# Cross-attention with a mixture-of-experts layer: the second k product moved directly behind the first in TensorE's order

## The chip, the cores and the metric

One core of one Trainium2 chip runs the whole program. The metric is the device time of one execution in microseconds (us); the median of three runs of the kernel before is 1068.2 us (1066.75 to 1069.43).

## The reference, cut to what matters

The input x is 16 batches of 256 tokens by 512. Each batch attends to its own context of 256 tokens by 256: 240 ordinary tokens and 16 further ones (DCA) that have their own weights and their own softmax. There are 16 heads of 32. The queries, and the keys, are normalised head by head. Then a layer with 6 experts follows, of which each batch uses 2.

```python
q = _ln((x @ Wq + bq).reshape(b, s1, H, HD), qn_w, qn_b)
kv = jnp.concatenate([y_main @ Wk + bk, y_main @ Wv + bv], axis=-1)
kv = kv.reshape(b, s2, H, 2 * HD)
k = _ln(kv[..., :HD], kn_w, kn_b)
v = kv[..., HD:]
ctx = _attn(qT, k.transpose(0, 2, 1, 3), v.transpose(0, 2, 1, 3))
ctx_dca = _attn(qT, k_dca.transpose(0, 2, 1, 3), v_dca.transpose(0, 2, 1, 3))
x = x + (ctx + ctx_dca) @ Wo + bo
x = x + ffn(_layernorm(x))       # gate on the batch's mean, 2 of 6 experts
```

## The kernel before, in words

**Two phases.** The function attention_phase works through the 16 batches one after the other, and ffn_phase then does the experts. The change lies in the first.

**A software pipeline.** In one step of the attention phase, TensorE does the attention of batch b, and between its pieces the projections (q, k, v) of batches ahead, so that the other engines have time to work on the scores. The function walk (line 328) lists the steps: p0, p1, p2 fill the pipeline; first, body (eleven times), close and late have both attention and projections; later, last and tail empty it. So there are fourteen steps in which attention (attn) and projections (proj) are both done. The Python function body (line 745) of the TensorE program is the order of TensorE's work, written out by hand. Each engine has such an order of its own and takes its instructions strictly in that order; semaphores make one engine wait for another.

**The attention of a batch.** First come eight groups of scores (line 679, matmuls at line 687) with the queries on the partitions; VectorE takes their maxima (line 1012), ScalarE their exponentials and sums (line 844). From the sums a shift for each query and head is made: VectorE (line 1121), TensorE transposes it (line 692, LT), VectorE splits it into s_hi and s_lo (lines 1123 and 1125), and two DMAs (line 377; s_hi issued by SyncE, s_lo by ScalarE) lay it as additional rows under the stacked queries QS. Then the scores are computed a second time, transposed and with the shift already in them: eight groups scores_t 0 to 7 (line 699, matmuls at line 708). I call them T0 to T7. T0 waits until both DMAs have landed (line 702). Each Tp fills one of two double-bank buffers, sc[p % 2], with four matmuls, and must wait until ScalarE has emptied that buffer (line 704). ScalarE empties it with one activation, exp, into pt (probabilities, line 855, activation at line 860): exps 0 to 7. Behind T3, T5 and T7 stand products of the probabilities with the values (line 713, matmuls at line 723), here P0, P1, P2, and at the end of the step P3.

**The k products.** project_kv(step, b, c, 0) computes half c of the key rows: K0 (128 rows) and K1 (112 rows), each of six matmuls of 512 columns (line 653), because the operands are split in a high and a low part. Results go to one of four PSUM banks (ring). K0 has bank 3, K1 has bank 0; the unit that used bank 0 ahead of K1 is LT. VectorE adds the bias and takes a bank's result away (bias_k, line 1061). ScalarE squares it (line 835), VectorE sums the squares (line 976), GpSimd takes the root (line 509) and normalises k (line 533); TensorE transposes it in the next step (line 674), before that step's fourth group of scores. ScalarE's order at this place is: exp 0, exp 1, square of K0, exp 2, exp 3, square of K1, exp 4, exp 5, exp 6, exp 7. VectorE's is: bias of K0, normalise first half of q (line 984), bias of K1, sum of K0's squares, normalise second half of q, result of P0 (line 1079), sum of K1's squares.

Of the kernel before, what the change touches and what calls it, by code (L numbers as in the profile page):

```python
# [169 lines left out]
def attention_phase(nc, stack, early, moe, x, ctx, Wq, bq, Wk, bk, Wv, bv, Wdca, bdca, qn_w, qn_b, kn_w, kn_b,  # L170
# [140 lines left out]
    def begin(eng, step, name, b):  # L311

        wait(eng, evac[u.bank(step, name)], u.count(step, name, b))
        return ring[u.bank(step, name)]
# [10 lines left out]
    def wait_evac(eng, step, name, b):  # L325
        eng.wait_ge(evac[u.bank(step, name)], u.count(step, name, b) + 1)
# [36 lines left out]
    def kv_half(columns, half):  # L363

        return columns.rearrange("p (h w) -> p h w", w=W)[:, :, half * HD:(half + 1) * HD]
# [212 lines left out]
    def _(pe):  # L578
# [33 lines left out]
        def x_transposes(step, b):  # L612
            pe.wait_ge(xh_rdy, T * (b + 3))
            for j in range(2):
                bank = begin(pe, step, f"XT{j}", b)
                for k in range(2):
                    for t in range(T):
                        last = pe.transpose(bank[:, (k * T + t) * P:(k * T + t + 1) * P],
                                            xh[:, t, (2 * j + k) * P:(2 * j + k + 1) * P], ident[:, :])
                last.then_inc(full[u.bank(step, f"XT{j}")], 1)  # L620

        def context_transposes(step, b):
            pe.wait_ge(c_ld, 16 * (b + 3))
            bank = begin(pe, step, "CT", b)
            for cc in range(CC):
                for c in range(NC):
                    last = pe.transpose(bank[:, cc * TOK + c * P:cc * TOK + (c + 1) * P],
                                        cin[:, c, cc * P:(cc + 1) * P], ident[:, :])
            last.then_inc(full[u.bank(step, "CT")], 1)

        def project_q(step, b, t):
            bank = begin(pe, step, f"Q{t}", b)
            wait_evac(pe, step, "XT0", b)
            wait_evac(pe, step, "XT1", b)
            if step == "p1":
                pe.wait_ge(prep, 2)
            for kc in range(KC):
                last = pe.matmul(bank[:, :], xT[:, kc, t * P:(t + 1) * P], wq[:, kc, :],  # L638
                                 start=(kc == 0), stop=(kc == KC - 1))
            last.then_inc(full[u.bank(step, f"Q{t}")], 1)  # L640

        def project_kv(step, b, c, half):

            name = "KV"[half] + str(c)
            bank = begin(pe, step, name, b)
            if half == 0:
                wait_evac(pe, step, "CT", b)
                if step == "p1":
                    pe.wait_ge(wkv_rdy, 2)
            parts = [(cc, c_part, w_part) for cc in range(CC)  # L650
                     for c_part, w_part in ((cT, wkv_hi), (cT, wkv), (cT_lo, wkv_hi))]
            for n, (cc, c_part, w_part) in enumerate(parts):
                last = pe.matmul(bank[0:ROWS[c], :], c_part[:, cc, c * P:c * P + ROWS[c]],
                                 kv_half(w_part[:, cc, :], half),
                                 start=(n == 0), stop=(n == len(parts) - 1))
            last.then_inc(full[u.bank(step, name)], 1)
# [11 lines left out]
        def k_transposes(step, b):  # L668
            pe.wait_ge(k_norm, NC * (b + 2))
            for j in range(2):  # L670
                bank = begin(pe, step, f"KT{j}", b)
                for g in range(2):
                    for c in range(NC):
                        last = pe.transpose(bank[:, g * TOK + c * P:g * TOK + c * P + ROWS[c]],
                                            kb[0:ROWS[c], c, (2 * j + g) * P:(2 * j + g + 1) * P],
                                            ident[0:ROWS[c], 0:ROWS[c]])
                last.then_inc(full[u.bank(step, f"KT{j}")], 1)

        def scores(b, par, k):

            if k == 0:
                pe.wait_ge(q_in, STACKED * (b + 1))
                pe.wait_ge(k_in, STACKED * (b + 1))
            wait(pe, sc_evac[k % 2], 8 * b + k // 2)
            t, quad = k // G, k % G
            for i in range(HP):
                last = pe.matmul(sc[k % 2][:, i // 2, (i % 2) * TOK:(i % 2 + 1) * TOK],  # L687
                                 QS[par][0:BLK, i, quad, t * P:(t + 1) * P], KS[par][0:BLK, i, quad, :],
                                 start=True, stop=True)
            last.then_inc(sc_full[k % 2], 1)  # L690

        def shift_transposes(step, b):
            bank = begin(pe, step, "LT", b)
            pe.wait_ge(lt_rdy, b + 1)
            for t in range(T):
                last = pe.transpose(bank[0:2 * H, t * P:(t + 1) * P], lt[:, t, :], ident[:, :])
            last.then_inc(full[u.bank(step, "LT")], 1)
# [31 lines left out]
        def out_projection(step, b, t, half):  # L729

            if half == 0:
                if step in ATTN:
                    pe.wait_ge(ctx_rdy, b)
                else:
                    wait_evac(pe, "last", "PV3", B - 1)
                bank = begin(pe, step, f"WO{t}", b)
            else:
                bank = ring[u.bank(step, f"WO{t}")]
            for g in (2 * half, 2 * half + 1):
                last = pe.matmul(bank[:, :], ot[:, g, t * P:(t + 1) * P], wo[:, g, :],  # L740
                                 start=(g == 0), stop=(g == G - 1), skip_group_check=True)
            if half == 1:
                last.then_inc(full[u.bank(step, f"WO{t}")], 1)

        def body(step, b, par):
            attn, proj, keyed, wout = step in ATTN, step in PROJ, step in KEYED, step in WOUT
            if attn:
                scores(b, par, 1)
            if keyed:
                project_kv(step, b, 0, 1)  # L750
            if attn:
                scores(b, par, 2)
            if keyed:
                project_kv(step, b, 1, 1)
                k_transposes(step, b)
            if attn:
                scores(b, par, 3)
            if wout:
                out_projection(step, b, 0, 0)
            if attn:  # L760
                scores(b, par, 4)
            if wout:
                out_projection(step, b, 0, 1)
            if attn:
                scores(b, par, 5)
            if wout:
                out_projection(step, b, 1, 0)
            if attn:
                scores(b, par, 6)
            if proj:  # L770
                x_transposes(step, b)
            if attn:
                scores(b, par, 7)
            if proj:
                project_q(step, b, 0)
                context_transposes(step, b)
            if wout:
                out_projection(step, b, 1, 1)
            if attn:
                shift_transposes(step, b)  # L780
            if proj:
                project_q(step, b, 1)
            if proj:
                project_kv(step, b, 0, 0)
            if attn:
                scores_t(b, par, 0)
                scores_t(b, par, 1)
            if proj:
                project_kv(step, b, 1, 0)
            if attn:  # L790
                scores_t(b, par, 2)
                scores_t(b, par, 3)
                values(step, b, par, 0)
                scores_t(b, par, 4)
                scores_t(b, par, 5)
                values(step, b, par, 1)
            if step == "p1":
                project_dca()
            if step == "p2":
                dca_k_transposes()  # L800
                scores(0, 0, 0)
            if proj:
                q_transposes(step, b)
            if attn:
                scores_t(b, par, 6)
                scores_t(b, par, 7)
                values(step, b, par, 2)
            if step in AHEAD and attn:
                scores(b + 1, 1 - par, 0)
            if attn:  # L810
                values(step, b, par, 3)
            if step == "p2":
                pe.wait_ge(wo_ld, 32)

        walk(pe, body)


# [846 lines left out]
```

## Time and profile before

| what | value |
|---|---|
| median of 3 runs | 1068.2 us (1066.75 to 1069.43) |
| the profiled execution | 1067.38 us |
| its span, first to last instruction | 1065.5 us, 17588 instructions |
| mean granted TensorE clock | 0.951 |
| TensorE matmuls busy | 926.1 us (87%) |
| TensorE weight loads busy | 658.8 us (62%) |
| VectorE busy | 765.5 us (72%) |
| ScalarE busy | 595.5 us (56%) |
| GpSimd busy | 393.8 us (37%) |
| steps with attention and projections | 14, from some 110 to 650 us |

The profiled execution gives the durations; its own time lies 0.8 us below the median of the runs. Engines in its rows: PE is TensorE's matmuls, PEld its weight loads, DVE VectorE, ACT ScalarE, POOL GpSimd, SP SyncE; a q behind a name means the engine's sequencer (a DMA issue, for example). "L653" is line 653 of the kernel. "x8" is the number of instructions merged in a row. What stands in square brackets is idle time of that engine before the row, and what ended it.

### The profile page before, as it was taken

Reading aid. Unit: us, or ns where it says so; the run is one execution under the profiler, and the core shown is the slowest. Engines: PE = TensorE matmul, PEld = TensorE weight load, DVE = VectorE, ACT = ScalarE, POOL = GpSimd, SP = SyncE. Lnnn points to the kernel's source line nnn. Section 1 sums busy time; section 2 is a strip of 40 time slices with the busy share of each in tenths; the row PEclk is TensorE's granted clock in tenths of the full one; section 3 lists DMA queues with packets and bytes.
Section 4 is the critical chain, followed back from the end, with each engine's and each line's share of the span. In section 5 each row is a group of like instructions: output and inputs, shape, how many; then the busy total and the mean of one; then the engine's idle time right before and its main releaser. Section 6 shows DMA issues by size and latency. Waiting matters only on the chain. (4 is left out here: it accounts for less than half of the span.)

```text
span 1065.5 us, 17588 instructions
## 1 busy us (share of the span) xinstructions
PE 926.1 (87%) x5148; PEld 658.8 (62%) x5148; DVE 765.5 (72%) x1723; ACT 595.5 (56%) x1627; POOL 393.8 (37%) x277
## 2 busy tenths in 40 slices
PE   3673999999999999999999997764599999999998
PEld 1343656556556655655655654432489999898997
DVE  6644788778777778777777776334877878878784
ACT  1134778678778678678678778554422323223231
POOL 4627537537536636636636744000000000000000
PEclk9796999999999999999999999777699999999999
DMA  9236455464464364365364355367011111111111
GB/s 273 39 81 152 109 128 136 122 145 123 115 157 118 107 170 114 98 170 119 92 172 117 90 147 120 96 239 234 1 60 60 59 56 42 59 59 59 59 39 40
DMA packets 54588, 116.54 MB, mean 109 GB/s; under 512 B 11992, under 2 KB 20568, under 8 KB 54296
## 3 DMA queue, kind: packets, MB, share of 16 engines
q1 hardware_dynamic: 53416, 115.29, 39.2%
q10 hardware_dynamic: 816, 0.79, 0.3%
q0 software_dynamic: 320, 0.02, 0.2%
q8 instruction: 18, 0.29, 0.1%
q14 instruction: 18, 0.15, 0.0%
HBM read 47.24 MB, written 17.30 MB: 61 GB/s over the span
## 5 line engine op out<-in xcount | busy, mean ns | idle before, releaser
L509 POOL TENSOR_TENSOR vs<-vs,neg_half 128x16 f32<-128x16 f32 x66 | 195.9, 2982 | 185.4 <-DVE vs L978 185.2
L851 ACT ACTIVATE sc<-sc,nm 128x240 f32<-128x240 f32 x512 | 225.8, 456 | 31.5 <-DVE ed L1023 31.5
L1018 DVE TENSOR_REDUCE pm<-sc 128x64 f32<-128x1024 f32 x128 | 156.4, 1222 | 49.9 <-PE sc L687 46.3
L860 ACT ACTIVATE pt<-sc 128x1024 f32<-128x1024 f32 x128 | 124.2, 1024 | 44.6 <-PE sc L708 44.6
L687 PE MATMUL sc<-KS,QS 96*128 96x256 f32 x512 | 99.4, 318 | 46.7 <-ACT sc L851 34.9
L1475 ACT ACTIVATE hb<-hb 128x352 f32<-128x352 f32 x64 | 31.9, 498 | 186.9 <-DVE hb L1531 186.8
L687 PEld LDWEIGHTS sc<-KS,QS 96*128 96x128 f32 x512 | 72.2, 194 | 101.8 <-ACT sc L851 75.8
L638 PE MATMUL ring<-wq,xT 128*128 128x512 f32 x256 | 121.3, 618 | 15.7 <-DVE q L1056 7.4
L740 PE MATMUL ring<-wo,ot 128*128 128x512 f32 x256 | 121.0, 597 | 0.7 <-DVE ot L1079 0.7
L851 ACT ACTIVATION_READ_ACCUMULATOR sc<-sc,nm 128x1 f32 x512 | 117.0, 229 | 0.0
L708 PE MATMUL sc<-QS,KS 100*128 100x256 f32 x512 | 82.6, 305 | 13.7 <-DMA QS<-s_lo 13.1
L708 PEld LDWEIGHTS sc<-QS,KS 100*128 100x128 f32 x512 | 70.7, 200 | 32.2 <-DMA QS<-s_lo 12.2
L638 PEld LDWEIGHTS ring<-wq,xT 128*128 128x128 f32 x256 | 47.8, 197 | 68.4 <-issue 55.9
L1349 PE MATMUL f_ring<-w_hi,f_xT_hi 128*128 x256 | 84.8, 331 | 2.6 <-DVE f_xT_lo L1513 2.6
L1405 PE MATMUL f_ring<-w_hi,hT_hi 128*128 (+1 forms) x192 | 80.7, 420 | 5.9 <-DVE w_lo L1503 5.7
L1349 PE MATMUL f_ring<-w_hi,f_xT_lo 128*128 x256 | 84.1, 328 | 0.0
L1349 PE MATMUL f_ring<-w_lo,f_xT_hi 128*128 x256 | 83.9, 328 | 0.0
L1405 PE MATMUL f_ring<-w_lo,hT_hi 128*128 (+1 forms) x192 | 76.1, 396 | 0.0
L1405 PE MATMUL f_ring<-w_hi,hT_lo 128*128 (+1 forms) x192 | 75.9, 395 | 0.0
L723 PE MATMUL ring<-pt,v 128*32 128x256 f32 x1024 | 70.6, 394 | 0.6 <-ACT pt L860 0.6
L1079 DVE TENSOR_SCALAR ot<-ring,bv_p 128x256 f32<-128x256 f32 x64 | 30.7, 479 | 50.9 <-PE ring L723 50.9
L1335 POOL TENSOR_TENSOR gd<-euler,gd 128x1 f32<-128x1 f32 x16 | 8.8, 552 | 156.4 <-DVE gd L1611 156.4
(154 smaller groups left out, 1858.3 us busy)
## 6 DMA issues: line engine op xcount, KB each, us to landing
QS<-q_hi SPq DMA_DIRECT2D x128, 128.0 KB, 2.3
KS<-k_hi SPq DMA_DIRECT2D x128, 128.0 KB, 2.4
xin<-in_x_dram SPq DMA_DIRECT2D x16, 512.0 KB, 3.6
QS<-q_lo SPq DMA_DIRECT2D x64, 128.0 KB, 2.3
KS<-k_lo SPq DMA_DIRECT2D x64, 128.0 KB, 2.3
xres<-in_x_dram SPq DMA_DIRECT2D x16, 512.0 KB, 3.2
x_scratch<-xres SPq DMA_DIRECT2D x16, 512.0 KB, 3.8
x<-x_scratch SPq DMA_DIRECT2D x16, 512.0 KB, 3.2
```

The costliest lines, as they stand in the source:

```text
L509: pool.tensor_tensor(w, w, neg_half[0:rows, :], ALU.pow).then_inc(rstd, 1)
L638: last = pe.matmul(bank[:, :], xT[:, kc, t * P:(t + 1) * P], wq[:, kc, :], start=(kc == 0), stop=(kc == KC - 1))
L687: last = pe.matmul(sc[k % 2][:, i // 2, (i % 2) * TOK:(i % 2 + 1) * TOK], QS[par][0:BLK, i, quad, t * P:(t + 1) * P], KS[par][0:BLK, i, qu ...
L708: last = pe.matmul(sc[p % 2][:, i, c * S:(c + 1) * S], KS[par][:, h, g, c * P:(c + 1) * P], QS[par][:, h, g, :], start=True, stop=True)
L723: last = pe.matmul(bank[i * HD:(i + 1) * HD, 0:S], v[par][:, c, h * HD:(h + 1) * HD], pt[g % 2][:, i, c * S:(c + 1) * S], start=(c == 0), ...
L740: last = pe.matmul(bank[:, :], ot[:, g, t * P:(t + 1) * P], wo[:, g, :], start=(g == 0), stop=(g == G - 1), skip_group_check=True)
L851: last = act.activation(s, s, ACT.Exp, bias=nm[:, t, h:h + 1], accum_out=den[:, t, h:h + 1])
L860: act.activation(pt[g % 2][:, (p % 2) * 2:(p % 2) * 2 + 2, :], sc[p % 2][:, :, :], ACT.Exp).then_inc(sc_evac[p % 2], 1)
L1018: dve.tensor_reduce(pieces, s.rearrange("p h (c n) -> p h c n", n=DCA), AX_X, ALU.max, negate=True).then_inc(g_max, 1)
L1349: last = pe.matmul(bank[:, 0:FF], xT[xp][:, kc, t * P:(t + 1) * P], w1[wp][:, bass.ds(ex[e], 1), kc, :].rearrange("p a f -> p (a f)"), sta ...
L1405: last = pe.matmul(bank[:, :], hT[hp][0:rows, e, fc, t * P:(t + 1) * P], w2[wp][0:rows, bass.ds(ex[e], 1), fc, :].rearrange("p a n -> p (a ...
L1475: act.activation(hb[:, n, :], hb[:, n, :], ACT.Gelu).then_inc(h_rdy, 1)
```

## The change

Two lines are moved: project_kv(step, b, 1, 0), that is K1, comes directly behind K0 and ahead of T0. So the order K0, T0, T1, K1, T2, T3 becomes K0, K1, T0, T1, T2, T3. Nothing else changes: neither the work, nor the banks, nor the semaphores' counts, nor the order of another engine. In p1 and p2, which have no attention, K1 was behind K0 already.

```diff
             if proj:
                 project_kv(step, b, 0, 0)
+                project_kv(step, b, 1, 0)
             if attn:
                 scores_t(b, par, 0)
                 scores_t(b, par, 1)
-            if proj:
-                project_kv(step, b, 1, 0)
-            if attn:
                 scores_t(b, par, 2)
                 scores_t(b, par, 3)
                 values(step, b, par, 0)
```

## Rows read from the trace of the kernel before

**Rows 1.** The page: TensorE's busy time, and its granted clock in 40 slices

```profile
PE 926.1 (87%) x5148; PEld 658.8 (62%) x5148; DVE 765.5 (72%) x1723; ACT 595.5 (56%) x1627; POOL 393.8 (37%) x277
...
PEclk9796999999999999999999999777699999999999
```

**Rows 2.** Busy time in two whole steps: stretch, length, PE, PEld, DVE, ACT, POOL, clock

```profile
392.60:431.93 39.33, 37.03 (x215) 22.90 (x214) 30.61 (x66) 30.28 (x88) 22.11 (x12) 1.00 0.50 129
431.93:471.67 39.74, 37.03 (x215) 22.86 (x214) 30.24 (x66) 30.28 (x88) 22.08 (x12) 1.00 0.50 128
```

**Rows 3.** Groups of instructions, 110 to 640 us: busy us, mean ns, idle before

```profile
L860 ACT ACTIVATE pt<-sc 128x1024 f32<-128x1024 f32 x110 | 106.7, 1025 | 23.3 <-PE sc L708 23.3
...
L708 PE MATMUL sc<-QS,KS 100*128 100x256 f32 x440 | 66.9, 292 | 3.6 <-DMA QS<-s_lo 3.5
...
L1061 DVE TENSOR_TENSOR kb<-ring,bkv_b 128x512 f32<-128x512 f32 (+1 forms) x28 | 19.3, 690 | 7.4 <-PE ring L653 7.4
```

**Rows 4.** Timeline of TensorE, one step: start us, duration us, what

```profile
435.46 0.40 PE L653 MATMUL ring<-wkv_hi,cT_lo 128*128 128x512 f32 x1
436.47 1.21 PE L708 MATMUL sc<-QS,KS 100*128 100x256 f32 x8 [0.61 <-DMA QS<-s_lo]
437.51 0.40 PE L653 MATMUL ring<-wkv_hi,cT 128*112 128x512 f32 x1
...
438.71 0.40 PE L653 MATMUL ring<-wkv_hi,cT_lo 128*112 128x512 f32 x1
438.94 1.10 PE L708 MATMUL sc<-QS,KS 100*128 100x256 f32 x8
439.98 1.07 PE L723 MATMUL ring<-pt,v 128*32 128x256 f32 x16
440.98 1.36 PE L708 MATMUL sc<-QS,KS 100*128 100x256 f32 x8
```

**Rows 5.** Timeline of ScalarE: the issue of s_lo's DMA in three consecutive steps

```profile
392.60 0.63 ACTq L377 DMA_DIRECT2D QS<-s_lo  x1
...
431.93 0.63 ACTq L377 DMA_DIRECT2D QS<-s_lo  x1
...
471.67 0.63 ACTq L377 DMA_DIRECT2D QS<-s_lo  x1
```

**Rows 6.** Timeline of TensorE: T0 and T1 of the step before that of rows 4

```profile
396.71 1.22 PE L708 MATMUL sc<-QS,KS 100*128 100x256 f32 x8 [0.18 <-DMA QS<-s_lo]
```

**Rows 7.** Timeline of ScalarE in the step of rows 4

```profile
437.24 1.94 ACT L860 ACTIVATE pt<-sc 128x1024 f32<-128x1024 f32 x2 [1.07 <-PE sc L708]
439.07 0.63 ACT L835 ACTIVATE sq<-kb 128x512 f32<-128x512 f32 x1
439.62 1.94 ACT L860 ACTIVATE pt<-sc 128x1024 f32<-128x1024 f32 x2
441.44 0.63 ACT L835 ACTIVATE sq<-kb 112x512 f32<-112x512 f32 x1
441.96 1.95 ACT L860 ACTIVATE pt<-sc 128x1024 f32<-128x1024 f32 x2
```

**Rows 8.** Timeline of TensorE in the step late: K0's last matmul, then T0

```profile
632.27 0.40 PE L653 MATMUL ring<-wkv_hi,cT_lo 128*128 128x512 f32 x1
632.54 1.22 PE L708 MATMUL sc<-QS,KS 100*128 100x256 f32 x8
```

**Rows 9.** K1's consumers after rows 4: VectorE, GpSimd, k's transposes (first to last start)

```profile
439.14 0.69 DVE L1061 TENSOR_TENSOR kb<-ring,bkv_b 112x512 f32<-112x512 f32 x1 [0.83 <-PE ring L653]
...
440.71 6.14 POOL L509 TENSOR_TENSOR vs<-vs,neg_half 128x16 f32<-128x16 f32 x2 [0.63 <-DVE vs L978]
446.93 2.06 POOL L533 TENSOR_TENSOR kb<-kb,vs 128x512 f32<-128x512 f32 x2
...
L674 PE MATMUL ring<-ident,kb x8: 260/267/274, 452.6 to 453.3; 128*128 128x128 f32 x4, 112*128 112x112 f32 x4
```

**Rows 10.** Timeline of TensorE in the step later, which has no projections

```profile
670.29 2.08 PE L708 MATMUL sc<-QS,KS 100*128 100x256 f32 x8 [4.87 <-DMA QS<-s_lo]
```

## The prediction

> **What bounds the kernel now.** I began with the page. It shows TensorE's matmuls busy for 87% of the span [rows 1], which tempts one to take TensorE for the bound everywhere. The change acts only where attention and projections are mixed, in fourteen steps, so I next asked for whole steps, cut from one issue of the DMA of s_lo to the next. In both, TensorE is busy for 37.03 us and ScalarE for 30.28 us, yet one lasts 39.33 us and the other 39.74 us [rows 2]. The work is the same and the length is not: something that is no engine's work decides 0.41 us.
>
> The timelines of the two steps show what. In the first, T0 starts at 396.71, which is 4.11 us after the issue of s_lo at 392.60; in the second it starts at 436.47, 4.54 us after the issue at 431.93 [rows 4 to 6]. T0 is 0.43 us later in the second, and that step is 0.41 us longer. In both, the wait that ends last ahead of T0 is the landing of s_lo. So a delay of T0 goes through to the end of the step one to one. That is the central reading: **the start of T0 is on the path**, for all that TensorE looks nearly full.
>
> ScalarE's timeline shows why. It idles 1.07 us for T0's result; then it runs exps 0 and 1, the square of K0, exps 2 and 3, the square of K1 and exps 4 and 5 with no idle time between the rows [rows 7]. Whatever moves exp 0 moves this whole train. T5 can start only when exp 3 has emptied its buffer, and everything in TensorE's order behind T5 follows.
>
> **The change part by part.**
>
> K1 ahead of T0. Its six matmuls start at 437.51, and the next matmul behind them starts at 438.94 [rows 4]: 1.43 us for the six, 0.24 us for each. In fourteen steps that is 14 x 1.43 = 20.0 us put ahead of T0. The operands of K1 are those of K0 but for the rows, and both banks are free. LT, which used bank 0 before, was taken away by VectorE before s_lo's DMA could be issued, 3.5 us before K0's last matmul starts [rows 4, 5], so I expect no wait ahead of K1.
>
> For one matmul of 512 columns I take the row's 0.24 us. The Trainium skill, page "TensorE: Matmul & The Clock Gate", section "Back-to-back issue gap", gives 518 cycles at 2.4 GHz, that is 0.216 us; by it K1 would cost 1.30 us and the sum would come out 1.8 us lower. The pitch measured here is longer, so the measurement decides.
>
> What K1 covers. While TensorE waits for s_lo's landing it can now do K1. In all steps together TensorE idles 3.6 us ahead of line 708 [rows 3], and I counted such a wait in eleven of the fourteen steps. The idle time is counted from the modelled end of K0's last matmul, 0.40 us after its start, whereas a following matmul may start 0.24 us after it, as T2 does behind K1 (438.71 to 438.94 [rows 4]). So each of the eleven waits is really 0.16 us longer: 11 x 0.16 = 1.8 us. The three steps without idle time (one is the step late [rows 8], where T0 starts 0.27 us after K0's last matmul) add some 0.3 us. Covered in all: 3.6 + 1.8 + 0.3 = 5.7 us. The rest of K1, 20.0 - 5.7 = 14.3 us, delays T0: 1.02 us in the mean step. After the change no step should wait for s_lo: K1 ends 1.43 us after the point where T0 could start at the earliest, and the longest wait seen is 0.61 + 0.16 = 0.77 us [rows 4].
>
> What K1's old slot gives back. T2 started 2.47 us after T0 and K1 stood ahead of it. T2 needs sc[0], which exp 0 empties: exp 0 starts at 437.24 and lasts 1.025 us [rows 3, 7], so T2 could start at about 438.3 instead of 438.94, 0.6 us earlier. That helps only if exp 2 was waiting for T2. ScalarE had its own train: exp 1, then the square of K0, then exp 2. The square to the next exp takes 0.55 us here (439.07 to 439.62) and 0.52 us at the second square (441.44 to 441.96) [rows 7]; the difference, 0.03 us, is all that exp 2 can have waited. The price is bounded by 0 and by 14 x 0.6 = 8.5 us; I take 14 x 0.03 = 0.4 us, since ScalarE shows no idle time there, and keep the other end for a rival.
>
> New waits. T2 now waits for exp 0 and T3 for exp 1, where K1 used to fill the time; together they idle TensorE for as much as K1 no longer fills, about 1 us. Queued behind T2 and T3 are P0, T4 and T5. P0 needs exp 1 and T4 needs exp 2, which the delayed train ends later in any case, so this costs nothing further. If ScalarE's train were shorter, P0 and T4 would be late next.
>
> K1's consumers. VectorE idled 0.83 us for K1 in this step [rows 9], 7.4 us in all [rows 3]. The bias of K1 now comes earlier, but VectorE's next instruction, the sum of K0's squares, needs ScalarE's square of K0, which comes 1 us later. GpSimd's roots start after that, so they shift by the same 1 us. I cost this at nothing. The cover is large: GpSimd ends with k at 448.99, and the transposes that need it start at 452.6 [rows 9], 3.6 us later; they shift too. No DMA is moved: SyncE's and ScalarE's issues of s_hi and s_lo come before, and the loads in SyncE's queue behind them depend on K0, K1, T0 in nothing.
>
> The sum: 20.0 - 5.7 - 0.4 = **13.9 us slower**. On the profiled execution's own 1067.38 us this gives 1081.3 us; the median of the runs stands 0.8 us above that execution, so I predict 1068.2 + 13.9 = 1082.1 us, 1.3% longer. The steps outside the fourteen, and the experts' phase, keep their length and shift as a whole.
>
> **The rivals.**
>
> Faster: TensorE is the bound of the whole step. Then the only thing that counts is its idle time, and K1 fills 5.7 us of it: 1068.2 - 5.7 = 1062.5 us. For it speaks the busy share, 37.03 of 39.33 us [rows 2]. It would decide if TensorE had no idle time behind T1, so that pulling K1 out of there advanced everything by K1's full 1.43 us; it turns to a gain from a relief of 1.02 us per step on. Against it: T2 cannot start before exp 0 ends, so the relief is at most 0.6 us, and a later T0 lengthened the step one to one though TensorE had the same work. The Trainium skill, page "Perfetto Trace Analysis", section "Identifying the Most-Contended Engine", says that matmul busy time is no good measure of TensorE's headroom and the busy share of weight loads a better one; that share is 22.90 of 39.33 us here, which speaks against this rival too. Chance 0.02.
>
> Partial relief: exp 2 was in truth paced by T2, and ScalarE's row hides it. Then 8.5 us come back instead of 0.4: 20.0 - 5.7 - 8.5 = 5.8 us slower, 1074 us. Against it stands the 0.55 beside the 0.52 us. Chance 0.04.
>
> No change: the delay is absorbed, because another chain (the next step's keys or stacked queries) ends the step just as late. Then 1068 us. Against it: the one-to-one lengthening between T0 and the next step, and a longer delay makes any other chain less binding, not more. That K1 still runs where it was isn't possible, as TensorE's order is the program's. Chance 0.02.
>
> The clock falls: TensorE's pauses grow, and in late parts of the trace its granted clock fell from the upper level (2.4 GHz) to the lower (1.2 GHz) [rows 1]. There the engine had sat idle for up to 4.87 us at a time [rows 10]. In the fourteen steps the new pauses are some 0.5 us each and the clock was granted in full [rows 2]. If each step lost, by a halved clock, its T0 to P0 stretch once more (3.5 us from T0 to P0 [rows 4]), that would be 14 x 3.5 = 49 us: 1131 us. Chance 0.02.
>
> **How the numbers follow.** The forecast has a chance of 0.90. Its own uncertainty: the six matmuls could be 1.30 us rather than 1.43 (-1.8 us), the first and the last of the fourteen steps might pass on less (-2 us), the handing over at T2 and T3 might cost 0.1 us per step (+1.4 us), and the runs scatter by 1.3 us. This gives 1078.5 to 1085 us, and what is left out of the range is less than 2 in 10. A difference under 0.3%, 3.2 us, is about what a measurement can't tell from no change. Slower by more than that: forecast, partial relief and clock, 0.96, from which I take 0.02 for what I have not thought of: 0.94. Faster 0.03, the same 0.03.
>
> **What would show it.** Right, if in the changed kernel the wait for s_lo ahead of line 708 is gone in all fourteen steps; T0 starts some 1.67 us (0.24 + 1.43) after the start of K0's last matmul in every step alike, which is 5.20 us after the issue of s_lo (435.46 - 431.93 + 1.67); the body steps all have nearly one length, 39.33 + (5.20 - 4.11) = 40.4 us; ScalarE's idle time ahead of exp 0 has grown by 1 us per step, from 1.07 to 1.7 us in the step read above [rows 7]; exps 0 to 5 keep their distances; small idle times appear on TensorE ahead of T2 and T3, ended by exp; and VectorE's 7.4 us for K1 are gone. Wrong, if exp 2 follows T0 by clearly less than the 3.15 us of now (439.62 - 436.47), if the steps keep their length though T0 is later, or if the granted clock shows a dip within the fourteen steps.

## The result, and the profile after

The changed kernel took 1082.55 us in the median of four runs (1080.23 to 1085.41), against 1068.59 us for the kernel before, measured beside it: a ratio of 1.0138, with a 95% interval of 1.0117 to 1.0159. That is 14.0 us more; 13.9 us were predicted. That the two agree to 0.1 us is luck, since the interval reaches from 12.5 to 17.0 us. The profiled execution took 1080.23 us, 12.85 us more than the one of before. Two executions of the experiments stand far outside the others, 1112.71 us in experiment 1 and 1849.24 us in experiment 5: the ratios leave them out, the medians don't.

What comes ahead of the fourteen steps scatters from run to run (they began between 117.2 and 122.1 us in the profiles of this study), so I also compare the fourteen steps alone: from the first issue of s_lo's DMA to the fifteenth. This is the view of one source line, line 377 of ScalarE, cut off behind the fifteenth issue; the last two times of a row are the first and the last start. First the kernel before, then the changed one.

```profile
L377 ACTq DMA_DIRECT2D QS<-s_lo x15: 621/627/757, 117.8 to 666.3; - x15
```

```profile
L377 ACTq DMA_DIRECT2D QS<-s_lo x15: 622/627/757, 117.9 to 679.3; - x15
```

The fourteen steps grew from 548.5 to 561.4 us, by 12.9 us. The whole difference of the profiled executions lies in them.

Whole steps of the changed kernel (columns as in [rows 2]):

```profile
399.78:440.06 40.28, 37.35 (x215) 23.08 (x214) 30.62 (x66) 30.23 (x88) 22.09 (x12) 1.00 0.49 126
440.06:480.32 40.26, 37.34 (x215) 23.08 (x214) 30.22 (x66) 30.21 (x88) 22.09 (x12) 1.00 0.49 126
```

Both last 40.3 us. The lengths that differed by 0.41 us in [rows 2] are now one, because nothing varies any more ahead of T0. The clock was granted in full. Over the whole fourteen steps, 117.9 to 679.3 us, the same view gives 1.00 too, and the page has a 9 (90% or more) in every slice from the fifth to the twenty-fifth:

```profile
PE 930.5 (86%) x5148; PEld 660.7 (61%) x5148; DVE 765.8 (71%) x1723; ACT 594.5 (55%) x1627; POOL 394.1 (37%) x277
...
PEclk9886999999999999999999999768689999999999
```

The groups that answer to [rows 3], 110 to 655 us (line 858 is line 860 of before, 1059 is 1061):

```profile
L858 ACT ACTIVATE pt<-sc 128x1024 f32<-128x1024 f32 x111 | 107.9, 1031 | 37.3 <-PE sc L708 37.3
L708 PE MATMUL sc<-QS,KS 100*128 100x256 f32 x448 | 72.7, 296 | 11.5 <-ACT pt L858 11.5
...
L1059 DVE TENSOR_TENSOR kb<-ring,bkv_b 128x512 f32<-128x512 f32 (+1 forms) x28 | 19.2, 687 | 0.0
```

TensorE no longer waits for s_lo; it waits 11.5 us for exps instead. VectorE's 7.4 us for K1 are gone. ScalarE's idle time ahead of exps 0 and 6 is 37.3 us. The 23.3 us of [rows 3] come from a window that ends before the last of the fourteen steps does; over exactly the fourteen steps it was 24.3 us. So it grew by 13.0 us, as much as the steps did: what the change added is idle time, not work.

TensorE in one step, behind [rows 4]:

```profile
443.58 0.40 PE L653 MATMUL ring<-wkv_hi,cT_lo 128*128 128x512 f32 x1
443.82 0.40 PE L653 MATMUL ring<-wkv_hi,cT 128*112 128x512 f32 x1
...
445.00 0.40 PE L653 MATMUL ring<-wkv_hi,cT_lo 128*112 128x512 f32 x1
445.24 1.11 PE L708 MATMUL sc<-QS,KS 100*128 100x256 f32 x8
447.00 0.74 PE L708 MATMUL sc<-QS,KS 100*128 100x256 f32 x4 [0.64 <-ACT pt L858]
447.91 0.74 PE L708 MATMUL sc<-QS,KS 100*128 100x256 f32 x4 [0.18 <-ACT pt L858]
448.58 1.07 PE L723 MATMUL ring<-pt,v 128*32 128x256 f32 x16
```

T0 starts 1.66 us after the start of K0's last matmul, and the two new waits stand ahead of T2 and T3, 0.82 us together. ScalarE in the same step, behind [rows 5, 7]:

```profile
440.06 0.63 ACTq L377 DMA_DIRECT2D QS<-s_lo  x1
...
445.92 1.94 ACT L858 ACTIVATE pt<-sc 128x1024 f32<-128x1024 f32 x2 [1.61 <-PE sc L708]
447.74 0.63 ACT L833 ACTIVATE sq<-kb 128x512 f32<-128x512 f32 x1
448.26 1.94 ACT L858 ACTIVATE pt<-sc 128x1024 f32<-128x1024 f32 x2
450.07 0.65 ACT L833 ACTIVATE sq<-kb 112x512 f32<-112x512 f32 x1
450.59 1.96 ACT L858 ACTIVATE pt<-sc 128x1024 f32<-128x1024 f32 x2
```

T0 starts 5.18 us after the issue of s_lo (445.24 - 440.06). Exp 0 follows T0 by 0.68 us, against 0.77 us in [rows 4, 7]; exp 2 follows exp 0 by 2.34 us, against 2.38 us. Exp 2 thus follows T0 by 3.02 us instead of 3.15 us; the prediction had named a clearly smaller distance as a sign that it was wrong, and this is a small part of that.

### The profile page after: what moved, and what is told of

Its sections match the earlier page's. It is cut to its first block and busy times, and to the rows that moved or that the text cites. A ratio compares the mean times of both kernels' runs of the same rounds, so it can differ in the third digit from the quotient of the medians.

```text
span 1078.4 us, 17588 instructions
## 1 busy us (share of the span) xinstructions
PE 930.5 (86%) x5148; PEld 660.7 (61%) x5148; DVE 765.8 (71%) x1723; ACT 594.5 (55%) x1627; POOL 394.1 (37%) x277
## 5 line engine op out<-in xcount | busy, mean ns | idle before, releaser
L740 PE MATMUL ring<-wo,ot 128*128 128x512 f32 x256 | 122.1, 601 | 0.7 <-DVE ot L1077 0.7
L708 PE MATMUL sc<-QS,KS 100*128 100x256 f32 x512 | 86.6, 306 | 21.5 <-ACT pt L858 12.0
L974 DVE TENSOR_REDUCE vs<-sq 128x16 f32<-128x512 f32 x66 | 45.0, 681 | 40.5 <-ACT sq L833 40.4
```

Source lines behind the costliest of these rows:

```text
L708: last = pe.matmul(sc[p % 2][:, i, c * S:(c + 1) * S], KS[par][:, h, g, c * P:(c + 1) * P], QS[par][:, h, g, :], start=True, stop=True)
L974: dve.tensor_reduce(w, squares(n, values), AX_X, ALU.add).then_inc(var_rdy, 1)
```

## The experiments

**1 and 2. K1 cut to one matmul, at the old and at the new place.** Both kernels have this edit; one is made in the kernel before, the other in the changed one. Most of k's second half is left out in them.

```diff
-                project_kv(step, b, 1, 0)
+                project_kv(step, b, 1, 0, cut=attn)
...
+            if cut:
+                parts = parts[:1]
```

> K1 is cut from six matmuls to one in the fourteen steps, at its old place behind T1 (so most of k's second half is left out). My theory: the old slot lies beside ScalarE's train of exps and costs nothing there; T2 can start 0.6 us earlier but exp 2 only 0.03 us earlier, so about 0.4 us less than the kernel before, 1067.8 us. Rival 'TensorE is the bound': five matmuls of 0.24 us in fourteen steps go, 16.7 us less, 1051.5 us. Rival 'partial relief' (exp 2 paced by T2): 0.6 us a step, 1060 us.

> K1 is cut to one matmul in the fourteen steps, at its new place ahead of T0 (most of k's second half is left out). My theory: what counts is T0's start. One matmul ends 0.24 us after K0, before s_lo has landed in ten of the steps, so T0 starts where it did in the kernel before: 1068 us, within 1 us, which is 14 us below the changed kernel. If the order itself (T2 directly behind T1, K1 in front) cost something else than the time of the matmuls, it would stay near 1082 us. Rival 'TensorE is the bound': clearly below 1060 us.

Measured: 1069.15 us at the old place, ratio to the kernel before 0.9999 (0.9982 to 1.0017); 1069.02 us at the new place, 0.9999 (0.9982 to 1.0016). Five of six matmuls were taken from TensorE in fourteen steps, 16.7 us of its work, and nothing came of it. This is the plainest evidence that TensorE's busy share doesn't set these steps. With one matmul in front of T0 the new order is as fast as the old, so the order as such costs at most some 2 us of the 13. The fourteen steps took 671.0 - 122.1 = 548.9 us and 669.6 - 119.3 = 550.3 us, against 548.5 us; one step in each (40.06 and 40.30 us) is 0.6 us longer than its T0 explains, and what held it up isn't shown. TensorE's timeline with the single matmul at the old place:

```profile
480.60 1.21 PE L710 MATMUL sc<-QS,KS 100*128 100x256 f32 x8
481.65 0.40 PE L655 MATMUL ring<-wkv_hi,cT 128*112 128x512 f32 x1
482.45 0.74 PE L710 MATMUL sc<-QS,KS 100*128 100x256 f32 x4 [0.40 <-ACT pt L862]
```

T2 (here line 710) starts 1.85 us after T0 instead of 2.47 us, as exp 0 allows. Exp 2 started 2.35 us after exp 0 (483.72 and 481.37) instead of 2.38 us: the relief at the old place is 0.03 us a step, not 0.6. The rivals "TensorE is the bound" and "partial relief" both fall here.

**3. K1 done twice ahead of T0,** in the changed kernel.

```diff
-                project_kv(step, b, 1, 0)
+                project_kv(step, b, 1, 0, times=2 if attn else 1)
...
-            for n, (cc, c_part, w_part) in enumerate(parts):
+            for n, (cc, c_part, w_part) in [item for _ in range(times) for item in enumerate(parts)]:
```

> K1's six matmuls are done twice in the changed kernel, ahead of T0. My theory: nothing is left to cover, so T0 and the step are later by all of the second six, 14 x 1.43 = 20.0 us, 1102.5 us. If a part of a later T0 is absorbed downstream, less than 20 us; half absorbed would be 1092 us.

Measured: 1101.59 us, ratio 1.0313 (1.0287 to 1.0339). That is 19.0 us above the changed kernel, by medians; its fourteen steps went from 118.8 to 700.4, that is 581.6 us, 20.2 us longer than in the changed kernel. Nothing of a later T0 is absorbed.

**4. The loads held back until both shift DMAs have landed,** in the kernel before.

```diff
+            if step in ATTN:
+                sp.wait_ge(sh_in, 32 * (b + 1))
             if step in STATS and step != "p0":
                 load_x(b + 4)
```

> The kernel before, in which SyncE issues the load of x, the store of the scratch and the two loads behind them only when both shift DMAs have landed. The lengths of its steps differed by the landing of s_lo, from 3.8 to 4.54 us after its issue. If packets of the load of x hold up s_lo's landing, T0 starts at 3.8 to 3.9 us in all steps (mean 4.17 before) and the kernel takes 4 to 5 us less, about 1064 us: T0's start is then shown to be on the path in the other direction too. If T0 is not on the path, or the landing has another cause, 1068 us. If the later loads themselves come late, slower than 1070 us.

Measured: 1066.6 us, ratio 0.9979 (0.9964 to 0.9994). Two consecutive steps; first ScalarE's three issues of s_lo and the two starts of T0:

```profile
393.53 0.63 ACTq L377 DMA_DIRECT2D QS<-s_lo  x1
...
397.39 1.21 PE L710 MATMUL sc<-QS,KS 100*128 100x256 f32 x8
...
432.21 0.63 ACTq L377 DMA_DIRECT2D QS<-s_lo  x1
...
436.30 1.21 PE L710 MATMUL sc<-QS,KS 100*128 100x256 f32 x8 [0.16 <-DMA QS<-s_lo]
...
471.53 0.63 ACTq L377 DMA_DIRECT2D QS<-s_lo  x1
```

T0 now starts 3.8 to 4.1 us after the issue, 3.93 us in the mean of fourteen (4.17 before). So what SyncE issues behind s_hi's DMA did hold up the start of T0 (the edit holds back the load of x and three more transfers and doesn't separate them), and an earlier T0 does shorten the kernel. The fourteen steps took 664.3 - 121.5 = 542.8 us, 5.7 us less; 14 x 0.24 = 3.4 us of it is T0. The whole kernel gained less than the 4 to 5 us expected, 2.2 us by medians, or 0.6 to 3.9 us by the interval: in the profile its fourteen steps began 3.7 us later, within the scatter named above. But the two steps above don't fit the one-to-one rule: T0 differs by 0.23 us (3.86 and 4.09), the lengths by 0.64 us (38.68 and 39.32). GpSimd and VectorE show the rest:

```profile
395.89 11.53 POOL L511 TENSOR_TENSOR vs<-vs,neg_half 128x16 f32<-128x16 f32 x4 [12.09 <-DVE vs L980]
...
434.57 5.79 POOL L511 TENSOR_TENSOR vs<-vs,neg_half 128x16 f32<-128x16 f32 x2 [12.28 <-DVE vs L980]
440.54 6.17 POOL L511 TENSOR_TENSOR vs<-vs,neg_half 128x16 f32<-128x16 f32 x2 [0.18 <-DVE vs L980]
```

```profile
401.72 0.70 DVE L986 TENSOR_TENSOR q<-q,vs 128x512 f32<-128x512 f32 x1 [0.17 <-POOL vs L511]
...
440.40 0.69 DVE L986 TENSOR_TENSOR q<-q,vs 128x512 f32<-128x512 f32 x1
```

In the first step the four roots run without a gap, 11.53 us; in the second they take 12.14 us with the gap. The difference, 0.61 us, is the step's. Only 0.18 us of it is the gap. The rest is the third root itself: it lasts 2.90 us in the first step, where it starts 0.07 us ahead of VectorE's normalisation of q (line 986), and 3.31 us in the second, where that instruction starts first. So a later T0 costs next to nothing up to some 3.9 us behind the issue, then 0.6 us at once. A train on GpSimd that I had costed at nothing was setting the length of the step.

**5 and 6. GpSimd's addition moved, in the kernel before and in the changed one.** Following GpSimd's row leads to VectorE's cast to q_hi, in the kernel before and in the step of [rows 9]. First GpSimd's last instruction of the step, then VectorE:

```profile
449.88 2.37 POOL L570 TENSOR_TENSOR xres<-xres,bo_b 128x1024 f32<-128x1024 f32 x1
```

```profile
451.23 1.58 DVE L1067 CAST q_hi<-qf 128x1024 fp32r<-128x1024 f32 x1
452.73 1.21 DVE L1018 TENSOR_REDUCE pm<-sc 128x64 f32<-128x1024 f32 x1
```

The addition ends at 452.25, the cast at 452.81, and the next group of maxima stands behind the cast. The like cast to k_hi takes 0.69 us. The Trainium skill, page "SBUF — State Buffer", section "Who interferes with whom", says that a cast in one of VectorE's two-port modes and a GpSimd instruction contend for a shared pair of ports under an exclusive lock, and that the one issued later blocks until the other is done. Whether this cast runs in such a mode no row here says; whether the addition holds it up can be tested. So the addition was moved behind q_low of the next step:

```diff
+        def add_bias(m):
+            pool.wait_ge(r_ld, 16 * (m + 1))
...
             if step in KEYED:
                 q_low(b + 1)
+            if step in WOUT:
+                add_bias(b - 1)
...
-            if step in ATTN:
-                pool.wait_ge(r_ld, 16 * (b + 1))
```

> The kernel before with one GpSimd instruction moved: the addition of the output bias to the residual (2.37 us) no longer closes GpSimd's step but comes behind q_low of the next step. New theory: the end of the step hangs on GpSimd's train (roots, k's normalisation, this addition) because VectorE's cast to q_hi ends 0.55 us after the addition in every step looked at, whenever it began, and takes 1.1 to 2.0 us where the like cast to k_hi takes 0.69 us. Then the cast takes 0.7 us, the third group of maxima comes 0.8 to 1.3 us earlier in each of fourteen steps, and the kernel takes 11 to 16 us less: 1053 to 1058 us. The theory of the prediction (TensorE's order behind T5 carries the delay, GpSimd has 3.6 us to spare): 1068 us.

> The same move in the changed kernel. If GpSimd's train is what carries T0's delay to the end of the step, it too gets 11 to 16 us faster, 1067 to 1072 us. Whether K1's new place still costs 13 us beside the kernel before with the same move tells if TensorE's own order carries the delay as well: if it does, the distance of the two stays 13 us; if GpSimd's train was the only carrier, the distance shrinks below 5 us.

Measured: 1060.23 us in the kernel before, ratio 0.99 (0.9861 to 0.9938), and 1069.62 us in the changed one, 1.0014 (0.9994 to 1.0034). The fourteen steps took 657.7 - 120.5 = 537.2 us and 671.3 - 121.2 = 550.1 us. VectorE in the first of the two kernels:

```profile
447.38 0.68 DVE L1070 CAST q_hi<-qf 128x1024 fp32r<-128x1024 f32 x1
447.98 1.22 DVE L1021 TENSOR_REDUCE pm<-sc 128x64 f32<-128x1024 f32 x1
```

The cast takes 0.68 us, which agrees with that rule of the Trainium skill, page "SBUF — State Buffer". Two things follow. GpSimd's train did end last, by about 0.8 us a step (11.3 us over the fourteen). And the two kernels still differ by 12.9 us in their fourteen steps, just as without the move, so something other than GpSimd's addition carries T0's delay as well. (Over the whole kernel they differ by 9.4 us in the medians and by 12.2 us in the ratios; one of the medians rests on few executions, three of them at 1056.0 to 1060.4 us.) It isn't the rest of GpSimd's train either, which now stands idle ahead of q_low until VectorE's cast is done:

```profile
448.15 2.38 POOL L519 TENSOR_TENSOR q_lo<-qf,q_hi 128x1024 fp32r<-128x1024 f32 x1 [2.12 <-DVE q_hi L1070]
```

I take it to be the train of TensorE and ScalarE, which I didn't follow to its end. So **two trains start at T0's exps and run side by side**; both shift by the same amount, and which of them ends last doesn't change the price of moving K1. My expectation for the first was 1053 to 1058 us; of the 0.94 us that the third group of maxima gained in the one step that I compared, the next waits gave back a part.

**7. Both holds together,** the addition moved and the loads held back, in the kernel before.

> The kernel before with the bias addition moved and with SyncE's loads held until both shift DMAs have landed. Both gains are in different parts of the step and should add up: 2 to 5 us below the first kernel of this set, about 1051 us.

Measured: 1054.8 us, ratio 0.9863 (0.9837 to 0.9888). This is the fastest kernel of the study, 13.5 us below the kernel before and 27.8 us below the changed one. Its fourteen steps took 652.9 - 118.8 = 534.1 us, 3.1 us less than with the addition moved alone: T0 came earlier by 0.20 us in the mean (3.96 against 4.16 us), 2.7 us in all, but the 2.3 us that had gone through GpSimd's train in experiment 4 didn't come again, as that train no longer ends last. By medians it lies 5.4 us below the kernel with the addition moved alone, slightly more than the 2 to 5 us expected. It stayed above 1051 us because that kernel had itself come out above its 1053 to 1058 us.

**8. Four of K1's matmuls ahead of T0, two behind T1,** in the kernel before.

```diff
                 project_kv(step, b, 0, 0)
+            if proj and attn:
+                project_kv(step, b, 1, 0, slice(0, 4))
...
-                project_kv(step, b, 1, 0)
+                project_kv(step, b, 1, 0, slice(4 if attn else 0, 6))
```

> The kernel before with the first four of K1's six matmuls ahead of T0 and the last two behind T1. T0 can then start 4.72 us after the issue of s_lo in every step, against a mean of 4.17 before and 5.19 after. T0's mean delay is 0.55 us; with 0.11 us back from T0's first weight load, which is hidden again behind K1, 14 x 0.44 = 6 us slower than before: 1074.5 us. If it is the splitting or the order that costs, not the time of the matmuls, 1082 us.

Measured: 1076.0 us, ratio 1.0073 (1.0047 to 1.01). T0 and the exps behind it, from TensorE's and ScalarE's timelines:

```profile
441.66 1.11 PE L709 MATMUL sc<-QS,KS 100*128 100x256 f32 x8
```

```profile
442.33 1.94 ACT L863 ACTIVATE pt<-sc 128x1024 f32<-128x1024 f32 x2 [1.14 <-PE sc L709]
```

T0 starts 4.71 us after the issue of s_lo in all fourteen steps, and exp 0 0.67 us after T0, as in the changed kernel and unlike the 0.77 us of before. The fourteen steps took 673.3 - 118.6 = 554.7 us, 6.2 us more than before, as expected. The price follows the number of matmuls that exceed the wait; neither splitting nor order costs anything of its own that shows.

**9. The loads held back in the changed kernel.** The edit is that of experiment 4.

> The changed kernel, with SyncE's loads held until both shift DMAs have landed. In the changed kernel K1 ends after s_lo's landing in every step, so an earlier landing can't move T0: T0 stays at 5.19 us after the issue of s_lo and the time at 1082 us, where the same hold took 0.2% off the kernel before. If a DMA still paces T0, it gets 2 us or more faster.

Measured: 1083.7 us, ratio 1.0148 (1.0115 to 1.0182); the fourteen steps took 678.8 - 117.2 = 561.6 us, as in the changed kernel (561.4). The landing of s_lo is off the path there.

**10. K1 done twice behind T1,** in the kernel before, with the edit of experiment 3.

> The kernel before, in which K1's six matmuls are done twice at the old place, behind T1. One K1 fills that place exactly: T2 starts 0.6 us later than exp 0 would allow and exp 2 begins 0.04 us after T2's end. So a second K1 delays exp 2 by all of its 1.43 us. But GpSimd's train hangs on the square of K0, which stands ahead of exp 2 and does not move; only TensorE's train is delayed, and it had 0.8 us to spare against GpSimd's. I expect 14 x (1.43 - 0.8) = 9 us, 1077 us. If both trains start behind exp 2, 20 us: 1088 us. If the old place has room for a second K1, 1068 us.

Measured: 1089.07 us, ratio 1.0195 (1.0164 to 1.0225); the fourteen steps grew by 20.3 us (686.7 - 117.9 = 568.8). I had expected 9 us, because GpSimd's train hangs on K0 and not on K1. VectorE's order makes it hang on K1 too:

```profile
450.34 0.68 DVE L984 TENSOR_TENSOR q<-q,vs 128x512 f32<-128x512 f32 x1
452.98 0.69 DVE L1061 TENSOR_TENSOR kb<-ring,bkv_b 112x512 f32<-112x512 f32 x1 [1.96 <-PE ring L653]
453.59 0.68 DVE L976 TENSOR_REDUCE vs<-sq 128x16 f32<-128x512 f32 x1
```

The sum of K0's squares, on which GpSimd's third root waits, stands behind the bias of K1 in VectorE's order. Exp 2 came 1.42 us later too, 3.80 us after exp 0 in the mean, so the other train was held up by as much. The old place behind T1 thus has room for one K1 and no more.

## Why the prediction was right

**The start of T0 is on the path: right.** It held when T0 was made later by K1 (12.9 us), by two thirds of K1 (6.2 us) and by two K1s (20.2 us more), and when it was made earlier (experiment 4). The evidence that I took from [rows 2, 4, 5, 6], two steps that differed by T0 alone, led to the right rule, but a pair was too little. In the ten steps from the third to the twelfth the time from the start of exp 0 to the next issue of s_lo is 34.45 us in the mean before and 34.42 us after, so there the rule holds one to one. The first two steps of the kernel before don't obey it. This is the second: ScalarE's issue, T0, GpSimd's roots without a gap, the next issue.

```profile
156.55 0.69 ACTq L377 DMA_DIRECT2D QS<-s_lo  x1
...
158.91 11.57 POOL L509 TENSOR_TENSOR vs<-vs,neg_half 128x16 f32<-128x16 f32 x4 [11.87 <-DVE vs L978]
...
160.47 0.74 PE L708 MATMUL sc<-QS,KS 100*128 100x256 f32 x4
...
195.29 0.65 ACTq L377 DMA_DIRECT2D QS<-s_lo  x1
```

T0 starts 3.92 us after the issue and the step lasts 38.74 us: 0.19 us less of T0 than in the first step of [rows 2], and 0.59 us less of length. It is the jump of experiment 4. In the changed kernel this step is 1.54 us longer, though its exp 0 starts only 1.18 us later.

**The price of K1, 1.43 us a step: right.** From 443.82 to 445.24 it is 1.42 us. The 0.216 us that the Trainium skill (page "TensorE: Matmul & The Clock Gate", section "Back-to-back issue gap") gives for a single matmul of 512 columns would have made it 1.30 us, by estimate; the trace has 0.24 us at the new place as well.

**What K1 covers, 5.7 us: right.** T0 started at 4.17 us in the mean before and 5.19 us after, 14 x 1.016 = 14.2 us where 14.3 us was predicted.

**What comes back, 0.4 us: too small, and for another reason.** Exp 2 did gain its 0.03 us, but GpSimd's train leaves ScalarE's at the square of K0, ahead of exp 2, so by the order of the instructions that gain shouldn't shorten the step; no run separates it from the 0.03 us between 34.45 and 34.42 us. What clearly came back is in T0 itself. Behind a wait its first matmul is followed only 0.22 us later by the second (436.47 and 436.69 in the step of [rows 4]), behind K1 by the usual 0.12 us. I take this for the first weight load: behind K1 it starts 0.23 us ahead of the matmul (438.71 for T2 in the kernel before), behind the wait only 0.01 us ahead of it (436.46 for T0). Exp 0 thus came 0.10 us sooner after T0 in each step, some 1.4 us in all. I had not costed it. 14.2 - 1.4 = 12.8 us, against 12.9 us measured in the fourteen steps. Part of that agreement is luck: the first two steps grew by 0.7 us more together than their exp 0 was delayed, the last two by 0.4 us less and the ten between them by 0.3 us less.

**"K1's consumers: costed at nothing, 3.6 us to spare": the number right, the reason wrong.** I looked for GpSimd's train only at k's transposes, where it has the 3.6 us. Its last instruction, the addition, holds up VectorE's cast to q_hi, and there it had less than nothing to spare: it ended the step, as experiments 4 and 5 show. The price of the change wasn't touched, since this train starts at T0's exps like the other. I had written that everything in TensorE's order behind T5 carries the delay. In both kernels the train that ended last was the one that I had missed; the other, which experiments 5 and 6 show to be delayed as much, ended 0.8 us a step earlier. That the two shift alike kept the sum right, and I hadn't foreseen it.

**The rivals.** Experiments 1 and 2 exclude the TensorE bound and the partial relief; 3 and 8 exclude that a delay is absorbed; the clock was granted in full (1.00) in the fourteen steps.

## What to carry to other kernels

Work moved into a wait is free only up to the wait's length, and even then gains nothing unless its old place was on the path: here 0.4 us of wait per step was filled with 1.43 us of work, and the old place had hidden all of it. When two steps of one trace do the same work in different times, take their difference apart first; it gives the price of a delay without an experiment. Then look whether the other steps obey it: here the first two of the fourteen did not, and they pointed to the train on GpSimd. Follow each train of an engine to its very last instruction, and ask what another engine can't do while that one runs.

## What the runs showed of the hardware

VectorE's cast of 128x1024 from fp32 to fp32r between two SBUF tensors took 0.68 us when GpSimd was idle (experiment 5) and 1.58 us while a GpSimd addition of 2.37 us ran; it ended 0.56 us after the addition's end, whether it had begun 1.0 us or 1.4 us before that end. In the median of sixteen it took 1.58 us in the kernel before.

GpSimd's third root of a step (128x16) took 2.90 us where it started ahead of VectorE's normalisation of q (128x512) and 3.27 to 3.45 us where that one had started first or at the same time, in all 168 steps of the twelve profiles.

The DMA of s_lo carries 32 KB. A load of 512 KB issued 1.7 us after it, and the transfers behind that load, delayed the start of T0, which waits for s_lo, by 0.24 us in the mean of fourteen steps (experiment 4).
